# Products with a spectrum, at four frequencies: two of them moved from VectorE to GpSimd

## What is computed

```python
Kf = jnp.fft.rfft(K, n=n, axis=-1)
xf = jnp.fft.rfft(x, n=n, axis=1)
y = jnp.fft.irfft(xf * Kf.T[None], n=n, axis=1)[:, :L]
return y + x * D_skip
```

## Time and profile before

| | us |
|---|---|
| median of 3 runs | 1694.19 |
| lowest, highest | 1694.01, 1695.35 |
| the profiled execution's own time | 1691.25 |
| its span | 1689.1 |
| PE busy in it | 1330.4 (79%) |
| DVE busy in it | 929.4 (55%) |
| POOL busy in it | 327.1 (19%) |

### The profile page before, as it was taken

One profiled execution on the slowest core, in us unless ns is written; L12 is line 12 of the kernel. 1 busy time (PEld: TensorE's weight loads), 2 busy tenths in 40 slices (PEclk: granted clock), 3 DMA queues, 4 the chain that ended last, 5 costly groups with the idle time before them and its releaser, 6 DMA issues. The chain is left out here.

```text
span 1689.1 us, 17636 instructions
## 1 busy us (share of the span) xinstructions
PE 1330.4 (79%) x5358; PEld 810.5 (48%) x5358; DVE 929.4 (55%) x3400; ACT 480.8 (28%) x823; POOL 327.1 (19%) x592
## 2 busy tenths in 40 slices
PE   0265669699889979979988997997995551999997
PEld 0245434345545555455554554545543240667674
DVE  6955414777576567666757656766666428211111
ACT  0433201214322521621532342162142223332221
POOL 3210100203101120320320112022022120433322
PEclk9995779799979969979997996997996675899999
DMA  8000020020020020002003002001200005243511
GB/s 261 2 0 1 2 63 15 14 50 15 14 76 16 12 78 15 1 26 64 16 13 77 16 13 76 14 1 23 54 1 26 1 32 183 67 116 82 144 17 21
DMA packets 44856, 72.55 MB, mean 43 GB/s; under 512 B 8085, under 2 KB 26648, under 8 KB 44634
## 3 DMA queue, kind: packets, MB, share of 16 engines
q1 hardware_dynamic: 38618, 62.90, 12.7%
q0 software_dynamic: 6144, 8.52, 2.9%
HBM read 58.31 MB, written 13.11 MB: 42 GB/s over the span
## 5 line engine op out<-in xcount | busy, mean ns | idle before, releaser
L770 POOL TENSOR_SCALAR ve<-mv 128x2 f32<-128x2 f32 x80 | 18.1, 227 | 854.1 <-DVE mv L868 853.9
L1283 PE MATMUL ps<-x,keys 128*128 128x512 f32 x256 | 137.1, 662 | 11.1 <-DVE hT L954 11.1
L1283 PE MATMUL ps<-zT_second,w 128*128 128x512 f32 x256 | 119.1, 602 | 3.7 <-ACT big L1249 2.4
L1366 PE MATMUL ps<-hT,values 128*128 128x512 f32 x256 | 119.1, 593 | 0.0
L1809 PE MATMUL experts_ps<-experts_yT,experts_fc 128*128 128x512 f32 x256 | 113.5, 602 | 1.3 <-ACT experts_yT L1732 1.3
L1283 PE MATMUL ps<-w,big 128*128 128x256 f32 x512 | 113.6, 381 | 0.8 <-ACT big L1249 0.8
L1821 PE MATMUL experts_ps<-experts_fc,experts_hT 128*128 128x256 f32 x512 | 112.1, 380 | 0.8 <-ACT experts_hT L1744 0.8
L1283 PEld LDWEIGHTS ps<-w,big 128*128 128x128 f32 x512 | 96.6, 190 | 22.7 <-issue 8.5
L1821 PEld LDWEIGHTS experts_ps<-experts_fc,experts_hT 128*128 128x128 f32 x512 | 96.6, 190 | 14.7 <-ACT experts_hT L1744 1.6
L437 PE MATMUL pk<-setup_WA,setup_U 128*32 128x16 f32 x512 | 27.9, 214 | 93.5 <-DVE setup_WA L346 93.5
L1707 DVE SCALAR_TENSOR_TENSOR experts_o<-experts_ps,experts_wh,experts_b2w 128x256 f32<-128x256 f32 x32 | 15.5, 484 | 140.2 <-PE experts_ps L1821 140.2
(11 more groups left out here) (382 smaller groups left out, 2590.7 us busy)
## 6 DMA issues: line engine op xcount, KB each, us to landing
gT<-expert_gates SPq DMA_DIRECT2D x16, 1024.0 KB, 9.7
experts_fc<-in_fc1T SPq DMA_DIRECT2D x8, 1024.0 KB, 5.4
experts_fc<-in_fc2T SPq DMA_DIRECT2D x8, 1024.0 KB, 9.6
expert_table<-tb SPq DMA_DIRECT2D x8, 528.0 KB, 12.2
x<-in_x SPq DMA_DIRECT2D x8, 512.0 KB, 3.5
xT<-in_xT SPq DMA_DIRECT2D x8, 512.0 KB, 3.6
out_x<-x SPq DMA_DIRECT2D x8, 512.0 KB, 11.5
w<-in_W SPq DMA_DIRECT2D x2, 1024.0 KB, 13.5
```

The source lines that it names most:

```text
L770: nc.gpsimd.tensor_scalar(o, i, c, None, ALU.add).then_inc(*tick(*event))
L1283: last = nc.tensor.matmul(o, l, r_, start=start, stop=stop)
L1366: last = nc.tensor.matmul(bank("O2", k), S["values"][:, c, k * P:(k + 1) * P], hT[:, c % RING, :], start=(c == 0), stop=(c == HC - 1))
```

## The change

In `product`, VectorE does j = 0 and 2 only, and GpSimd gets a `product` stage with the same five instructions for j = 1 and 3. The even ones use `prod[0]`, the odd ones `prod[1]`. The counting semaphore `spectrum_steps` becomes one for even and one for odd frequencies. New waits: GpSimd waits for `A3` before its product, each engine waits for its own `ys` of the product before (the buffer is the same), and `unfold` waits for `ys` of both 2 and 3.

```diff
-    y.declare("spectrum_steps", [(k, j) for j in range(FQ) for k in ("t1", "t2", "yc", "ys")])
+    y.declare("spectrum_even_steps", [(k, j) for j in (0, 2) for k in ("t1", "t2", "yc", "ys")])
+    y.declare("spectrum_odd_steps", [(k, j) for j in (1, 3) for k in ("t1", "t2", "yc", "ys")])
...
+            def product(b, j):
+                if j % 2 == 0:
+                    return
+                g.wait_ge(*at(b, "A3"))
+                a = high[:, j, :].rearrange("p (a d) -> p a d", a=2)
+                o = prod[1]
+                if j == 3:
+                    g.wait_ge(*at(b, "ys", 1))
+                nc.gpsimd.tensor_tensor(o[:, 0, :].rearrange("p (a d) -> p a d", a=2), a, S["kf"][:, j, :, :], ALU.mult).then_inc(*tick("t1", j))
+                nc.gpsimd.tensor_tensor(o[:, 1, 0:D], a[:, 0, :], S["kf"][:, j, 1, :], ALU.mult)
+                nc.gpsimd.tensor_tensor(o[:, 1, D:2 * D], a[:, 1, :], S["kf"][:, j, 0, :], ALU.mult).then_inc(*tick("t2", j))
+                g.wait_ge(*at(b, "t1", j))
+                nc.gpsimd.tensor_tensor(low[:, j, 0:D], o[:, 0, 0:D], o[:, 0, D:2 * D], ALU.subtract).then_inc(*tick("yc", j))
+                g.wait_ge(*at(b, "t2", j))
+                nc.gpsimd.tensor_tensor(low[:, j, D:2 * D], o[:, 1, 0:D], o[:, 1, D:2 * D], ALU.add).then_inc(*tick("ys", j))
...
             def product(b, j):
+                if j % 2:
+                    return
                 if j == 0:
                     v.wait_ge(*y.last(b, "table_stored"))
                 v.wait_ge(*at(b, "A3"))
                 a = high[:, j, :].rearrange("p (a d) -> p a d", a=2)
-                o = prod[j % 2]
+                o = prod[0]
+                if j == 2:
+                    v.wait_ge(*at(b, "ys", 0))
...
             def unfold(b):
-                v.wait_ge(*at(b, "ys", FQ - 1))
+                v.wait_ge(*at(b, "ys", 2))
+                v.wait_ge(*at(b, "ys", 3))
```

More of the change, by code:

```diff
@@ L854, in scores @@
                 multiply_small(tnm2[:, ts], tnm[:, ts], tv[:, ts], "tnm2", h)
-            trips(g, {"norm": norm_first, "attend": attend, "gates": gates, "rows": rows, "norm_ffn": norm_ffn, "ffn": ffn,
+            trips(g, {"product": product, "norm": norm_first, "attend": attend, "gates": gates, "rows": rows, "norm_ffn": norm_ffn, "ffn": ffn,
                       "norm_out": norm_out, "scores": scores})
```

## The result

| us | before | after |
|---|---|---|
| runs of this comparison | 1694.01 to 1697.18 (4) | 1705.04, 1709.04, 1709.11, 1709.34 |
| median | 1694.77 | 1709.07 |
| profiled execution, span | 1691.25, 1689.1 | 1709.04, 1707.2 |
| PE, DVE, POOL busy | 1330.4, 929.4, 327.1 | 1340.0, 939.8, 407.4 |

The medians differ by 14.3 us, where 9.2 were forecast. The ratio of the times on record is 1.0075, 95% interval 1.0059 to 1.0091, which is 10.0 to 15.4 us. Three of the four runs of before are those of the table ahead of the prediction; over the fourth, 1697.18, the change costs 11.9 us. The intervals overlap between 10 and 11 us.

A forecast was written before the change was run, and what follows sets the result against it. PE, busy 79% of the span, was taken as the bound, with its waits for relu 2 and `turn_back` deciding. Steady trips 6.7 plus last trip 2.5 gave 9.2 us over 1694.19: 1703.4 us, range 1697.5 to 1712.

The forecast's parts named there:

- Turns instruction by instruction: In the products, DVE and GpSimd instructions reading SBUF alternate whole, each costing its own duration less about 0.14 us.
- Relu 2 behind product 0 is what costs: In seven steady trips stretched product 0 delays relu 2, and so PE's H 4, by 0.96 us: 6.7 us in all.
- `unfold` 1.1 us late and hidden: In a steady trip `unfold` starts 1.1 us later, yet relu 4 and `R1` still reach PE in time.
- The last trip 2.5 us: With nothing beside the products there, alternating engines need 10.36 us instead of 7.90, 2.5 us more.
- Rivals 1 to 3: For the products: side by side (1692.2 us, 0.09); DVE keeps its turn (1705.8, 0.14); no handover saving (1714.7, 0.08).
- the saving at a handover: When DVE and GpSimd alternate, about 0.14 us of each instruction is spent while it waits for the other's end.
- the fourth rival: PE's longer pause might lower its granted clock; costed at nothing, chance 0.03 with other effects of this kind.
- rivals 2 and 3: In the products: DVE keeps its turn, starving GpSimd, 1705.8 us, chance 0.14; no saving between turns, 1714.7 us, chance 0.08.

The follow-up runs named there:

- e1: Kernel before the change plus four unused 512-column GpSimd tensor_tensor, inputs in SBUF, behind `A3` of each batch: 1746.16 us, before 1695.54.
- e2: Kernel before the change plus eight unused 512-column GpSimd memsets, which only write, behind `A3` of each batch: 1695.79 us, before 1695.54.
- e4: The changed kernel with relu 2 moved ahead of product 0 in VectorE's order: 1698.48 us, 2.9 over the kernel before.
- e6: The change with product 1 given back to VectorE, so only product 3 is on GpSimd: 1692.71 us, 0.7 over the kernel before.
- e10: The change in the last trip only, VectorE doing all four products in the seven steady trips: 2.7 us over the kernel before (1.0017).
- e9: The change itself run again in a later set of runs: 8.6 us over the kernel before (1.0051).
- e7: Kernel before the change plus one unused 256-column VectorE multiplication ahead of relu 2 in seven steady trips, delay 0.34 us: -0.3 us (0.9997).
- e3: Kernel before the change plus unused 512- and 256-column VectorE multiplications ahead of relu 2 in seven steady trips, delay 0.94 us: +9.7 us (1.0062).
- e8: Kernel before the change plus two unused 512- and two 256-column VectorE multiplications ahead of relu 2 in seven steady trips, delay 1.88 us: +31.4 us (1.0188).

## Why the prediction was right, and where it was short

- **Turns instruction by instruction**: right. A pair costs 0.87 us, no handover adds a pause, and 256 columns on GpSimd alone take 0.72. e1 and e2 show the cause, a two-input instruction of DVE beside one of GpSimd that reads SBUF. The price of 115 ns per handover that the Trainium skill gives, measured there on descriptor writing (SBUF — State Buffer, "A bandwidth-pool intuition that's wrong"), would by an estimate, added twice to the forecast's 0.86, have made a pair 1.09 us. The trace does not agree with it for this kind of turn.
- **Relu 2 behind product 0 is what costs**: right. 0.90 us per trip for the forecast 0.96, so 6.3 us for 6.7. GpSimd took its first turn 0.09 us after `A3`'s end instead of 0.20, which is more than the difference. e4 takes the cost away by the order alone.
- **`unfold` 1.1 us late and hidden**: 1.16, and PE waits for neither relu 4 nor `R1`. e6 hides 0.36 as well.
- **The last trip 2.5 us**: 2.55, and e10 has 2.7 us in all.
- **Rivals 1 to 3** fall: no overlap (0.94 instead of 0.42), no turn kept by DVE, and the saving at a handover is there in every pair.
- **The step that was short** is the fourth rival: the clock at nothing, with 0.03 for all effects of its kind. Two arguments stood for it, a half-idle window at 1.00 and the short pause. The matmuls right behind the pause do keep their clock, as argued. But the delay shifts everything behind it, and stretches at the lower clock appear 25 and 60 us behind the wait, or move. It was worth 4.0 us in the profile after, under 1 in e9's, and minus 2.6 by e7's median. I had read one window of one trip, and asked only what the pause does at its own place.
- **The total**: forecast 1703.4; the change's nine runs lie from 1703.43 to 1709.34 us. The surplus of the first four (14.3 for 9.2) is thus the clock's scatter in part; the waits alone explain 8.8. Of the remainder 0.5 us is the slower matmuls of the last trip. The range held 1709 because it had been stretched upward for rivals 2 and 3, neither of which happened; that this also covered the clock is luck.

What stays open: why a shift by a microsecond moves the low-clock stretches from one trip to the next, so why e3 runs at 1700 and at 1709 us. And why the experts' part starts some 3.5 us later on chip 3 than on chip 5: the wait is found, the sender of its signal is not, and no kernel of mine was aimed at it.

## What to carry over

Before work goes from VectorE to GpSimd, look whether VectorE's instructions beside it have two inputs in SBUF: then the engines alternate whole instructions if GpSimd's read SBUF too, and here two finished the four products later than one alone. What that costs is set by who waits for the last of them, so the order of the queue comes first: one relu moved ahead of the products was worth more than their division. A delay of an engine whose clock is throttled needs an error bar of its own, which a single profile cannot give.

## What the runs showed that I had not expected

- A delay's cost is not in proportion to it: 0.34, 0.94 and 1.88 us per trip gave -0.3, +9.7 and +31.4 us.
- Four matmuls of 512 columns took 1.98 us behind a pause of 1.30 (7 of 7) and 3.25 to 3.60 us behind one of 2.23 (4 of 7). In e8 the granted clock had fallen by then.
- Eight memsets of 512 columns on GpSimd beside VectorE's products cost neither engine anything: 0.42 us per 256 columns on VectorE, 0.99 per pair of memsets.
- The same kernel's part behind the last `A3` took 380.5 us on chip 5 and 386.1 on chip 11, and one pause in it was 0.27, 2.5 or 3.3 us by the chip.
